# Quaternion attention: grouping of score and value products, and square turns on VectorE

## The reference, cut to what matters

```python
q = quat_norm(quat_linear(x, qW, qb))
k = quat_norm(quat_linear(x, kW, kb))
v = quat_linear(x, vW, vb)
scores = jnp.einsum('bthd,bshd->bhts', q_, k_) * scale      # 16 heads, Dh = 16
scores = scores + jnp.mean(jnp.sin(J[:T])) * 0.1
attn = jax.nn.softmax(scores, axis=-1)
out = jnp.einsum('bhts,bshd->bthd', attn, v_).reshape(B, T, D)
return quat_linear(out, oW, ob)                              # added to x
```

## Time and profile before

| | us |
|---|---|
| median of 3 runs | 2855.62 (2854.02 to 2856.45) |
| span of the profiled execution | 2853.6 |
| TensorE busy in it | 2763.5 (97%) |
| VectorE busy | 1833.6 (64%) |
| ScalarE busy | 1632.5 (57%) |
| first to last exponential of the loop | 1994.1 to 2582.4 |

### The profile page before, as it was taken

How to read it: one execution, slowest core, us unless ns; L and a number is a source line. 1 busy time by engine, 2 the same in 40 slices (tenths; PEclk the granted TensorE clock), 3 DMA queues, 4 the chain that set the end, 5 groups by cost and what they waited for, 6 DMA issues and landing times.

```text
span 2853.6 us, 56389 instructions
## 1 busy us (share of the span) xinstructions
PE 2763.5 (97%) x23301; PEld 2159.3 (76%) x23301; DVE 1833.6 (64%) x3730; ACT 1632.5 (57%) x2473; POOL 556.2 (19%) x479
## 2 busy tenths in 40 slices
PE   9999999998999999999999988998999999998998
PEld 7888999996767778889999966996343434333998
DVE  8775555548887787755555467886545464436786
ACT  4534555543443455344555433776887888892786
POOL 0002224221000000021333155563000000001454
PEclk9999999999999999999999999999999999999999
DMA  5123333332000022233433264874442353413676
GB/s 170 64 67 115 95 90 83 88 95 68 2 3 24 3 71 82 67 103 86 100 86 85 77 168 125 212 209 111 107 127 52 86 100 91 102 38 120 185 213 149
DMA packets 237312, 279.77 MB, mean 98 GB/s; under 512 B 23267, under 2 KB 218496, under 8 KB 237056
## 3 DMA queue, kind: packets, MB, share of 16 engines
q1 hardware_dynamic: 204992, 229.78, 27.4%
q0 software_dynamic: 30720, 45.85, 8.6%
q10 hardware_dynamic: 1344, 0.53, 0.1%
HBM read 204.58 MB, written 72.88 MB: 97 GB/s over the span
## 4 chain that ended last, share of the span: by engine, by line
PE 81%; DVE 12%; issue 3%; ACT 3%; POOL 1%; DMA 1%; DVEq 0%; POOLq 0%; ACTq 0%
PE PS L162 18%; PE PS L164 18%; PE PS L163 18%; PE PS L3117 13%; PE PS L1086 6%; PE PS L170 2%; DVE SM L194 1%; PE PS L178 1%; DVE SM L1466 1%; PE PS L520 1%; DVE FW L671 1%; POOL out_dram L2561 1%; PE PS L3210 1%; DVE PROD L659 1%; ACT P L3267 0%
## 5 line engine op out<-in xcount | busy, mean ns | idle before, releaser
L3267 ACT ACTIVATE P<-PS 128x1024 f32<-128x1024 f32 x512 | 484.6, 1043 | 85.4 <-PE PS L3117 83.6
L162 PE MATMUL PS<-FH,FW 128*128 128x366 f32 (+1 forms) x1408 | 502.4, 357 | 1.3 <-DVE FW L671 1.2
L164 PE MATMUL PS<-FH,FW 128*128 128x366 f32 (+1 forms) x1408 | 497.3, 353 | 0.0
L163 PE MATMUL PS<-FH,FW 128*128 128x366 f32 (+1 forms) x1408 | 496.4, 353 | 0.0
L572 ACT ACTIVATE FHH<-PROD 128x366 fp32r<-128x366 f32 (+1 forms) x352 | 194.6, 553 | 413.3 <-DVE PROD L659 413.2
L162 PE MATMUL PS<-FW,FHH 128*122 128x256 f32 (+1 forms) x1184 | 338.3, 286 | 1.5 <-DVE FHH L666 1.5
L163 PE MATMUL PS<-FW,FHH 128*122 128x256 f32 (+1 forms) x1184 | 332.3, 281 | 0.0
L164 PE MATMUL PS<-FW,FHH 128*122 128x256 f32 (+1 forms) x1184 | 331.7, 280 | 0.0
L659 DVE TENSOR_TENSOR PROD<-SIL,PS 128x366 f32<-128x366 f32 (+1 forms) x352 | 206.7, 587 | 170.9 <-PE PS L164 167.2
L666 DVE TENSOR_TENSOR FHH<-PROD,FHH 128x366 fp32r<-128x366 f32 (+1 forms) x352 | 208.8, 593 | 140.5 <-ACT FHH L572 140.2
L162 PEld LDWEIGHTS PS<-FH,FW 128*128 128x128 f32 x1408 | 265.2, 188 | 23.0 <-issue 3.0
(11 more groups left out here) (485 smaller groups left out, 5556.1 us busy)
## 6 DMA issues: line engine op xcount, KB each, us to landing
WS<-L_ffn_w_dram SPq DMA_DIRECT2D x256, 256.0 KB, 3.5
WST<-L_ffn_W_dram SPq DMA_DIRECT2D x168, 256.0 KB, 3.4
S<-parts_scratch SPq DMA_DIRECT2D x60, 384.0 KB, 7.8
parts_scratch<-PT SPq DMA_DIRECT2D x28, 512.0 KB, 3.8
WST<-L_ffn_W1s_dram SPq DMA_DIRECT2D x40, 256.0 KB, 2.7
WST<-L_ffn_W3s_dram SPq DMA_DIRECT2D x40, 256.0 KB, 3.5
WST<-L_ffn_W2s_dram SPq DMA_DIRECT2D x40, 256.0 KB, 3.9
xa_scratch<-X SPq DMA_DIRECT2D x17, 512.0 KB, 5.1
```

The source lines that it names most:

```text
L162: e.matmul(o, lh, rh, start=start, stop=False, skip_group_check=True)
L163: e.matmul(o, ll, rh, start=False, stop=False, skip_group_check=True)
L164: return e.matmul(o, lh, rl, start=False, stop=stop, skip_group_check=True)
L3267: e.activation(self.PR[K % 3][:, 2 * jj:2 * jj + 2, :].rearrange("p a b -> p (a b)"), c.pair(2 * ((2 * K + jj) % 3)), ACT.Exp, scale=0.25) ...
```

## The change

1. Score products are issued in groups of three (one for each pair of PSUM banks) instead of two in each step. In turns K with K % 3 of 0 or 1 a group stands, in turns with K % 3 = 2 none; so three turns still hold six score products. Value products follow a group as soon as both their scores belong to earlier groups: two steps in one turn, one in the next, in turn.
2. `ft` and `fb` leave TensorE. `oc` becomes a VectorE transpose (32x32 squares) of bank 6 into OC; `ft` divides in that layout into tile TN; `fb` is a second VectorE transpose from TN to ONT, once per two head groups.
3. That leaves the channels in another order, so the rows of the output weights are copied once into WOP in this order, by 8 small DMAs on SyncE (`wp`), which wait for the last `vv` of batch 0. That `vv` moves two turns ahead, before the `put` and `stk` behind it.

```diff
-        self.ON, self.ONT = pl("ON", [128, 8, 256]), pl("ONT", [128, 2, 1024])
+        self.TN = [pl(f"TN{k}", [128, 16, 32]) for k in range(2)]
+        self.WOP, pad = pl("WOP", [128, 2, 256]), pl("PAD", [128, 512])
+        self.ONT = pl("ONT", [128, 2, 1024])
...
-        rest.add(1, ("sta", n, 0, 0, 1))
+        rest.add(1, ("sta", n, 0, 0, 1), ("vv", n, 0, 3), ("xb", n, 0), ("wp", n))
         rest.add(1, ("sta", n, 0, 1, 1), ("put", n, 0), ("stk", n, 1))
-        rest.add(1, ("vv", n, 0, 3), ("xb", n, 0))
...
-            if K < NK:
-                put(("qk", n, K, 0), ("qk", n, K, 1))
-            k = K - 2
-            if k >= 0:
-                put(("pv", n, k))
-                if k % 8 == 7:
-                    self.finish(fin, put, k // 8, K)
+            if K % 3 < 2:
+                first = 3 * (2 * (K // 3) + K % 3)
+                put(*[("qk", n, m // 2, m % 2) for m in range(first, min(first + 3, 2 * NK))])
+                while valued < NK and 2 * valued + 2 <= first:
+                    put(("pv", n, valued))
+                    valued += 1
+                    if valued % 8 == 0:
+                        self.finish(fin, put, valued // 8 - 1, K)
...
         fin.add(1, ("ft", n, u))
+        if u % 4 >= 2:
+            fin.add(0, ("fb", n, b, h, u // 4 % 2))
         if u % 8 >= 6:
-            for cc in range(2):
-                fin.add(1, ("fb", n, b, h, cc))
             for i2 in (2 * h, 2 * h + 1):
...
             w.wait_ge(*p.at("pvp", ("pv", n, 8 * u + 7)))
-            w.wait_ge(*p.at("pp", ("ft", n, u - 2) if u >= 2 else ("sta", n, 0, 1, 1)))
-            e.tensor_copy(self.OC[u % 2][:, :], c.bank(6)).then_inc(*p.one("ocv"))
+            if u >= 2:
+                w.wait_ge(*p.at("fv", ("ft", n, u - 2)))
+            e.transpose(self.OC[u % 2][:, :], c.bank(6)).then_inc(*p.one("ocv"))
         elif k == "ft":
...
+            bv = self.OC[u % 2][:, :].rearrange("p (t c) -> p t c", c=32)
+            w.wait_ge(*p.at("ocv", ("oc", n, u)))
+            w.wait_ge(*p.mine())
+            e.reciprocal(self.RC, bv[:, :, 16]).then_inc(*p.one("dv"))
+            w.wait_ge(*p.mine())
+            if u < 2:
+                w.wait_ge(*p.at("pp", ("vv", n, 0, 3)))
+            s0 = 16 * (g % 2)
+            e.tensor_tensor(self.TN[hf][:, :, s0:s0 + 16], bv[:, :, 0:16], self.RC.unsqueeze(2).broadcast_to([128, 16, 16]),
                             ALU.mult).then_inc(*p.one("fv"))
         elif k == "fb":
...
-            w.wait_ge(*p.at("pp", it))
+            w.wait_ge(*p.at("fv", ("ft", n, 8 * b + 4 * cc + 2 + h)))
             w.wait_ge(*p.at("pp", ("fo", n, b - 1, 2 * h + 1) if b else ("nn", n, 0, 0, 1)))
-            e.tensor_copy(self.ONT[:, cc, 512 * h:512 * h + 512], self.pb(it)).then_inc(*p.one("fv"))
+            e.transpose(self.ONT[:, cc, 512 * h:512 * h + 512],
+                        self.TN[h][:, :, :].rearrange("p t c -> p (t c)")).then_inc(*p.one("fv"))
...
+        elif k == "wp":
+            w.wait_ge(*p.at("pp", ("vv", n, 0, 3)))
+            self.k.ready(w, "vo")
+            for half in range(2):
+                for j in range(4):
+                    src, dst = 64 * half + 16 * j, 32 * j + 16 * half
+                    e.dma_start(self.WOP[dst:dst + 16], self.k.W["o"][src:src + 16]).then_inc(*p.dma("wp"))
```

More of the change, by code:

```diff
@@ L2834 @@
               "ht": {"pp": 1, "fv": 1}, "eb": {"eb": 1}, "sta": {"pp": 1}, "sq": {"sqv": 1}, "p1": {"prv": 1}, "qk": {"qkp": 1, "ex": 1},
[1 row of a table removed]
[1 row of a table added]
               "pj": {"pp": 1, "fv": 1}, "nn": {"pp": 1, "nra": 2}, "vv": {"pp": 1, "fv": 1}, "fo": {"pp": 1, "fv": 1}}
-    BANKED = ("ht", "pj", "nn", "vv", "ft", "fb", "fo", "sta")
+    BANKED = ("ht", "pj", "nn", "vv", "fo", "sta")
     NK = 256
@@ L2862, in __init__ @@
         A2 = c.place("A2", [128, 8, 4, 16], at=HIGH - 2048)
-        self.RC = c.sm(4, 4)
+        self.RC = c.sm(16)
         assert c.at <= c.top
@@ L2945, in on_pe @@
     def on_pe(it):
-        return it[0] in ("ht", "pj", "nn", "vv", "ft", "fb", "fo", "sta", "zt", "zg") or it[0] == "sk" and it[4] in (
+        return it[0] in ("ht", "pj", "nn", "vv", "fo", "sta", "zt", "zg") or it[0] == "sk" and it[4] in (
             (5, 6, 9) if it[3] == 0 else (1,))
@@ L2986, in order @@
         stacked, sunk, fin, ahead, sinking = 2, 0, Jobs(), Jobs(), Jobs()
+        valued = 0
         turns = [ahead, sinking]
@@ L3053, in plan @@
                 ring = self.early
-            elif it[2] == 3 and (k == "fb" and it[3] or k == "fo" and it[3] >= 2):
+            elif k == "fo" and it[2] == 3 and it[3] >= 2:
                 ring = self.late
@@ L3204, in pe @@
             ins.then_inc(*p.one("pvp"))
[L3205 to L3218, removed]
         elif k == "fo":
             b, i2 = it[2:]
-            self.k.ready(w, "vo")
+            w.wait_ge(*p.at("wp", ("wp", n)))
             w.wait_ge(*p.at("fv", ("fb", n, b, i2 // 2, 1)))
@@ L3226, in pe @@
                     ins = c.mm_by_columns(e, self.pb(it)[:, 256 * half:256 * half + 256],
-                                          self.ONT[:, q, 128 * i:128 * i + 128], self.k.W["o"][:, q, :], q == 0, q == 1)
+                                          self.ONT[:, q, 128 * i:128 * i + 128], self.WOP[:, q, :], q == 0, q == 1)
             ins.then_inc(*p.one("pp"))
@@ L3417, in dve @@
             b, g, hf = self.half(8 * u)
-            bv = self.pb(it).rearrange("p (t j c) -> p t j c", t=4, c=32)
-            w.wait_ge(*p.at("pp", it))
+            bv = self.OC[u % 2][:, :].rearrange("p (t c) -> p t c", c=32)
+            w.wait_ge(*p.at("ocv", ("oc", n, u)))
             w.wait_ge(*p.mine())
-            e.reciprocal(self.RC, bv[:, :, :, 16]).then_inc(*p.one("dv"))
+            e.reciprocal(self.RC, bv[:, :, 16]).then_inc(*p.one("dv"))
             w.wait_ge(*p.mine())
-            w.wait_ge(*p.at("pp", ("fb", n, b - 1, hf, 1) if b else ("vv", n, 0, 3)))
-            e.tensor_tensor(self.ON[:, 4 * hf:4 * hf + 4, 64 * g:64 * g + 64].rearrange("p t (j c) -> p t j c", j=4),
-                            bv[:, :, :, 0:16], self.RC.unsqueeze(3).broadcast_to([128, 4, 4, 16]),
+            if u < 2:
+                w.wait_ge(*p.at("pp", ("vv", n, 0, 3)))
+            s0 = 16 * (g % 2)
+            e.tensor_tensor(self.TN[hf][:, :, s0:s0 + 16], bv[:, :, 0:16], self.RC.unsqueeze(2).broadcast_to([128, 16, 16]),
                             ALU.mult).then_inc(*p.one("fv"))
```

## The result

| | before | after |
|---|---|---|
| median, us | 2855.28 | 2899.44 (2897.93 to 2901.63) |
| ratio | | 1.0157 [1.0145, 1.0169] |
| span of the profiled execution, us | 2853.6 | 2898.6 |
| first to last exponential of the loop, us | 588.3 | 632.2 |
| from there to the end, us | 271.2 | 269.1 |

Slower by 44 us. The forecast was +15 (2870), the range ended at 2892. The sign and the two main mechanisms (terms c and e) were right, the size was not: the forecast for the loop was some 606 us, it took 632. What failed is the allowance for all other waits, and terms a and g.

The account below looks back on a forecast made before the run. TensorE was taken to bound the loop as a whole (574 of 588 us). Terms -17 (a to c), +11 - 4, +26, -3.5, 0 and +2 for ScalarE's late restart gave +15 us, 2870 us; range 2842 to 2892.

Parts of the forecast that it names:

- Term c: Loop's score groups: without carry each takes the longer of ScalarE's 2.79 us and TensorE's work; loop 560 us, TensorE waiting 45.
- Term e: Jobs side by side on bank 7: the second waits until the first was read, 36 places, +26 us.
- Term a: 48 transpose groups of 0.58 us leave TensorE in the loop: 28 us less TensorE work.
- Term g: Weight copies on SyncE before the last put: 3.5 us of issue, taken as 0, up to 3 without cover.
- Term b: Fewer changes between score and value products on TensorE: three steps 4.62 us instead of 4.98, 31 us less.
- Term d: Unit ends, value product waiting for VectorE's read of bank 6: +11 us at 11 inside a pair, -4 at 20 others.
- The 11 us up to the 588 measured ... I leave as they are: Loop before: waits for VectorE and a DMA, 11 us between 577 and the measured 588, taken as unchanged.
- ScalarE's restart: Where a bare group of two value products restarts ScalarE late in the loop: +2 us.
- Term f: Kernel part after the loop's last copy: division and one transpose replace two transposes, less VectorE work in front; together -3.5 us.
- Rival 3: VectorE transpose slow, 1.4 us in place of 0.69: +18 to +25 us, 2890 us, chance 0.12.
- Rivals 1 and 2: 1: bank waits covered, 2844 us, chance 0.18. 2: groups carry, 2804 us, with part of bank waits 2820, chance 0.08.

Follow-up runs that it names:

- experiment 1: Halves apart: changed kernel with old product order, 2852.69 us, then also first batch's jobs in old places, 2845.68; kernel before with only the grouping, 2922.21.
- experiment 3: Exponentials from step 3 on over 512 of 1024 columns: changed kernel 2867.25 us, kernel before 2851.73 us; their distance falls from 44 to 15.5 us.
- experiment 4: Changed kernel, but a turn issues no value product behind a unit's last one: 2896.4 us; with jobs also between score group and value product, 2879.26 us.
- experiment 2: Changed kernel, from turn 12 the job of turns with K % 3 = 1 between score group and value product: 2878.93 us, ratio 1.0082.
- experiment 5: Changed kernel with the eight weight copies behind the last put and the stacking instead of in front: 2902.87 us, ratio 1.0162.
- the last version of experiment 1: Changed kernel with old product order, first batch's jobs in old places and weight copies behind them: 2845.68 us, repeated at 2845.41, ratio 0.997.

## Why the prediction was right in sign and wrong in size

- **Term a, transposes off TensorE (-28)**: failed as a size. The work is gone, but only 9 us of time (experiment 1), most likely because bare and half-bare steps belong to ScalarE. It stood in the sum only together with c, whose rule holds for that; on its own it would have misled.
- **Term b (-31)**: right, 4.64 us measured for 4.62.
- **Term c, the grouping takes the carry**: right in kind, shown by experiment 3. Summed over the 170 groups of the trace, the rule "the longer of 2.79 and TensorE's work" gives 547.5 us, 550.5 with the first and last exponentials, against 560 in the forecast. Other prices for the smallest jobs move up to 3 us between this sum and the later waits below.
- **Term d (+11 - 4)**: ten places at 1.04 as forecast; at the eleventh it cost 2.88, since the transpose started at 2272.70, some 1.9 us late, behind other operations in VectorE's queue. The ten groups that hold such an end and lie behind the start took 17.4 us over the rule. Removing the stops gives 3 (experiment 4).
- **Term e (+26)**: right in kind, 20.5 us by experiment 2; in size 35.6 us over the rule in the 35 groups with two jobs. The waits for the bank were priced well (0.91 above; a norm's, 1.20 by the trace at 2084.40). What was not in the sum is that such a group may have waited for ScalarE as well, and that VectorE is late where it has a block of small operations in hand (3.4 us over the rule at 2353.6, of which 2.19 by the trace are a wait for its `ZR`).
- **Term g (0)**: failed. The eight copies took 5.00 us of SyncE, not 3.5, and the stacking went out at 2031.05 in place of 2014.43. Counted from the loop's first exponential it went out after 20.3 us before, 33.8 in the changed kernel and 21.7 with the copies behind it (experiment 5): so 12 of the 13 us are the copies and their wait for `vv`. I had its need near 2032, so the cover was gone; the last of its data landed at 2042.68, TensorE waited 2.3 us for them and then ran at half clock (value products of 3.42 us at 2043.20). That group is 3.3 us shorter without the copies in front. The first two units took 38.0 us before and 47.8 after. In the kernel with the old order the early jobs cost 7 us in all.

```profile
2020.37 5.00 SPq L3477 DMA_DIRECT2D WOP<-Wo  x8
...
2031.05 1.77 SPq L3490 DMA_DIRECT2D S<-parts_scratch  x4
```

- **"The 11 us up to the 588 measured ... I leave as they are"**: the step that failed most. Waits that are no part of the rule came to 13.7 us in the first eleven groups (up to 2046) and 15.0 in later groups with one job or none, 28.7 together, where the forecast has 9 (11, less 4, plus 2 for ScalarE's restart). I estimate that some 9 of them are the lower clock (half of the 18.2 us that these groups spent at it), and most of the rest VectorE being late while TensorE has nothing else in hand: at 2314.85 an output product starts 2.32 us late, because the division and the transpose that it needs stand in VectorE's queue behind small operations of the gate.
- **Term f (-3.5)**: -2.1.
- **Rival 3, a slow transpose**: false, 0.716 and 0.711 beside the copy's 0.69. Rivals 1 and 2 are false with the sign.

The sum again, for the loop: 560 to 550.5 is -9.5; e +9.6; unit ends +6.4; other waits +19.7. Together +26, which is the 632 beside 606. The remaining 3 us are those by which the loop began later in this execution, in unchanged code, where between kernels it varied by 4.9 us.

What stays open: how the start's +9.8 us, of which 3.3 are the copies' in the traces, divides between the early `vv` and the clock in the grouped kernel. The old places can't be tried there, since the grouped value products come before the `vv` that they read.

## What to carry to other kernels

Before TensorE's work is cut or regrouped, ask which engine is the limit in each stretch: work removed is worth something only where it was the limit, and three buffers used as one group take away the carry that had evened dense and bare stretches out. Waits "left as they are" should be repriced whenever slack is removed, since each of them now stands on the path, and on TensorE it may be paid twice, the second time in clock. Value products that are put off to cover one wait can hold ScalarE's next buffer. Jobs that share one buffer need other work between them, and a moved DMA has to be followed to the transfer queued behind it.

## What the runs showed of the hardware that was not expected

- Waits of TensorE of about 1.5 to 2.9 us were followed by stretches at 1.2 GHz in some places and not in others, and the same wait of the same program in one execution and not in the next. At the lower level value products of 1.85 us took 3.54, and 20.5 us of it cost 9.5.
- The same program, profiled twice (the last version of experiment 1), had 10.2 and 3.4 us of it in its loop, and loops of 580.2 and 577.9 us.
- VectorE's transpose in 32x32 squares of 128x512 f32 takes 716 ns from PSUM and 711 from SBUF, a copy of that shape from PSUM 0.69 us.
- Eight DMAs from SBUF to SBUF took 5.00 us of issue on SyncE, 0.63 each, beside 0.44 for one of the four stackings (1.77 for four).
